# A graph network's last block: seven phases with barriers against one block of tile and chunk pipelines

## The reference, cut to what matters

```python
def _L3_gnn_ref(x, ...):                     # x here is h of the line below
    def _bn(x, gamma, beta):                 # over all nodes
        m = jnp.mean(x, axis=0)
        v = jnp.mean((x - m) ** 2, axis=0)
        return gamma * (x - m) * jax.lax.rsqrt(v + EPS) + beta
    def _hconv(x, src, dst, ew, w1, b1, w2, b2, g, b):
        h = jax.nn.relu(x @ w1 + b1)
        msg = ew[:, None] * h[src]
        agg = jax.ops.segment_sum(msg, dst, num_segments=x.shape[0])
        return jax.nn.relu(_bn(agg @ w2 + b2, g, b))
    residual = x
    h = _hconv(x, src, dst, hyperedge_weight, c1_w1, c1_b1, c1_w2, c1_b2, c1_g, c1_b)
    h = jax.nn.relu(_bn(h, bn1_g, bn1_b))
    h = _hconv(h, src, dst, hyperedge_weight, c2_w1, c2_b1, c2_w2, c2_b2, c2_g, c2_b)
    return jax.nn.relu(_bn(h, bn2_g, bn2_b) + residual)

x = x + _L2_gnn_ref(h, L2_gnn_weight, src, dst, edge_type_8, edge_weight)   # its sum over edges: relation aggregation
h = jnp.maximum(_layernorm(x, axis=-1), 0.0)
return x + _L3_gnn_ref(h, ...)
```

## Time and profile before

| | us |
|---|---|
| median of 3 runs | 4792.98 (4786.26 to 4800.61) |
| the profiled execution | 4766.33 |
| its span, first to last instruction | 4764.6 |
| mean granted TensorE clock, share of full speed | 0.704 |

### The profile page before, as it was taken

How to read it: one execution, slowest core, us unless ns; L and a number is a source line. 1 busy time by engine, 2 the same in 40 slices (tenths; PEclk the granted TensorE clock), 3 DMA queues, 4 the chain that set the end, 5 groups by cost and what they waited for, 6 DMA issues and landing times. The chain is left out here.

```text
span 4764.6 us, 64771 instructions
## 1 busy us (share of the span) xinstructions
PE 2346.9 (49%) x11287; PEld 1706.3 (36%) x11288; DVE 2095.4 (44%) x5420; ACT 1410.0 (30%) x4630; POOL 2382.3 (50%) x2445
## 2 busy tenths in 40 slices
PE   5301646566441155565565725555445555355555
PEld 2201534444330144444443313333323343233343
DVE  6502974444330089444447613335223333233344
ACT  2101746666530165666666600000200002000002
POOL 4774015555547500455553466663466660566660
PEclk9655977777665598777777956667666667666667
DMA  3443433333234344233325733331233330323320
GB/s 111 125 107 92 128 108 95 99 103 96 68 92 119 108 118 125 85 105 99 99 76 134 247 93 92 91 90 49 91 88 88 91 91 19 109 83 91 91 85 29
DMA packets 339577, 465.57 MB, mean 98 GB/s; under 512 B 108191, under 2 KB 253928, under 8 KB 336112
## 3 DMA queue, kind: packets, MB, share of 16 engines
q0 software_dynamic: 113824, 289.70, 21.3%
q1 hardware_dynamic: 157536, 109.12, 8.1%
q10 hardware_dynamic: 67956, 64.45, 4.8%
HBM read 385.88 MB, written 76.97 MB: 97 GB/s over the span
## 5 line engine op out<-in xcount | busy, mean ns | idle before, releaser
L153 POOL DMA_INDIRECT ring<-feat_d,srcC x784 | 755.3, 963 | 1065.2 <-ACTq L167 830.9
L153 POOL DMA_INDIRECT agc_ring<-feat_d,srcC x784 | 742.3, 947 | 614.6 <-SPq L312 234.9
L301 PE MATMUL agc_ps<-agc_ring,agc_hot 128*128 x1760 | 589.0, 500 | 594.2 <-issue 278.3
L175 ACT ACTIVATE ring<-ring,exC 128x64 f32<-128x64 f32 x3136 | 818.1, 336 | 137.1 <-issue 136.3
L301 PE MATMUL bank<-ring,arena 128*128 x1760 | 644.7, 502 | 114.3 <-ACT ring L175 46.7
L301 PEld LDWEIGHTS agc_ps<-agc_ring,agc_hot 128*128 128x128 f32 x1760 | 428.0, 254 | 755.1 <-issue 680.1
L910 PE MATMUL wide<-arena 128*128 128x100 bf16 x4704 | 273.9, 215 | 464.9 <-issue 253.2
L509 POOL DMA_INDIRECT attr_d<-abuf,attr_pos x392 | 406.8, 1038 | 191.2 <-issue 129.1
L228 DVE TENSOR_TENSOR acc<-acc,agc_ps 128x256 f32 x440 | 184.4, 419 | 685.7 <-DMA c1p_bias<-in_L_gnn_c_b 418.5
L153 POOL DMA_INDIRECT agr_ring<-rel_d,relC x392 | 371.3, 947 | 221.9 <-issue 107.9
L301 PEld LDWEIGHTS bank<-ring,arena 128*128 128x128 f32 x1760 | 400.9, 253 | 195.3 <-issue 141.8
(11 more groups left out here) (278 smaller groups left out, 2510.1 us busy)
## 6 DMA issues: line engine op xcount, KB each, us to landing
arena<-lo_d ACTq DMA_DIRECT2D x392, 128.0 KB
rel_d<-mid_stage SPq DMA_DIRECT2D x25, 1024.0 KB, 4.5
arena<-attr_d SPq DMA_DIRECT2D x98, 260.0 KB
abuf<-in_attr SPq DMA_DIRECT2D x56, 448.0 KB
ring<-feat_d,srcC POOLq DMA_INDIRECT x784
agc_ring<-feat_d,srcC POOLq DMA_INDIRECT x784
feat_d<-arena ACTq DMA_DIRECT2D x50, 128.0 KB
attr_d<-abuf,attr_pos POOLq DMA_INDIRECT x392
```

Of the source, the lines that this page charges most:

```text
L153: pool.indirect_dma_start(out=ring[:, u % RING, j, 0:D], out_offset=None, in_=table, in_offset=bass.IndirectOffsetOnAxis(ap=index[:, u, j: ...
L175: last = act.activation(part_of_row, part_of_row, ACT.Copy, scale=exC[:, bass.ds(u, 1), j, h])
L301: last = pe.matmul(ps[k % NHOT][:, 0:g.width], hot[:, k % NHOT, j, :], ring[:, slot, j, 0:g.width], start=(j == 0), stop=(j == 1))
```

## The change

Everything behind the middle stage becomes one function `tail()` with a single block, in which each engine runs one program from the relation aggregation to the output:

- The middle stage ends with DVE clearing `acc`; before the second convolution's aggregation POOL clears it, once its tiles have been turned. The relation aggregation adds its steps straight into `X`.
- All weights of both convolutions are loaded at the start of the block, by 16 DMAs of SP, and `AT` and `G` lie in the ring of the gathers.
- Layer norm, turn and the first projection form a pipeline by tile: each engine handles a different tile at a time, with two or three buffers between. The square root gets its epsilon as bias and is done per tile.
- A projection has a third matmul, of a row of ones (one contraction row) and the bias row, and ACT rectifies out of PSUM into the stage. DVE has no part in it.
- The convolution is a pipeline by chunk of 4 tiles (512 columns; 7 chunks, the last of one tile). ACT copies the turned even tiles and DVE the odd ones; ACT evicts, DVE takes the statistics of a chunk as soon as it is evicted. Normalisation is done chunk by chunk, with statistics, the next projection or the turning back behind it.
- At the output the drain goes and the two DVE operations of neighbouring tiles alternate.

The core of the diff (the functions `layer_norm`, `to_feature_major`, `conv_project`, `conv_finish` and the output block are removed):

```diff
                         dve.drain()
+                    dve.memset(acc[:, :, 0:D], 0.0)
 
     middle()
     end_phase()
+        CH = [(4 * r, min(4 * r + 4, NT)) for r in range(-(-NT // 4))]
+        AT = ring_flat[:, 0:KD * NP].rearrange("p (c n) -> p c n", c=KD)
+        G = ring_flat[:, KD * NP:2 * KD * NP].rearrange("p (c n) -> p c n", c=KD)
+        pt = [psum(f"t_pt{k}", [P, 512]) for k in range(2)]
+        pf = [psum(f"t_pf{k}", [P, 512]) for k in range(2)]
...
+        def act_rectify(act, z, n):
+            act.wait_ge(s_proj, NT * z + n + 1)
+            wait_from(act, stored[n % 5], 16 * (5 * z + n // 5))
+            act.activation(stage[:, n % 5, :], pf[n % 2][:, 0:D], ACT.Relu).then_inc(s_relu, 1)
+
+        def pe_project(pe, z, n, source):
+            wait_from(pe, s_relu, NT * z + n - 1)
+            pe.matmul(pf[n % 2][:, 0:D], ones[:, :], b1[:, z, :], start=True, stop=False)
+            for c in range(KD):
+                last = pe.matmul(pf[n % 2][:, 0:D], source(c), W1[:, z, c, :], start=False, stop=(c == KD - 1))
+            last.then_inc(s_proj, 1)
+
+        def dve_normalise(dve):
+            for j in range(NT + 1):
+                if j < NT:
+                    dve.bn_stats(stats[:, j, :], X[:, j, :])
+                if 1 <= j <= NT:
+                    dve.wait_ge(s_root, j)
+                    dve.reciprocal(rstd[:, j - 1:j], rstd[:, j - 1:j])
+                dve.drain()
+                if j < NT:
+                    dve.bn_aggr(mv[:, j, :], stats[:, j, :]).then_inc(s_var, 1)
+                if 1 <= j <= NT:
+                    dve.scalar_tensor_tensor(out=shift[:, j - 1:j], in0=mv[:, j - 1, 0:1], scalar=-1.0,
+                                             in1=rstd[:, j - 1:j], op0=ALU.mult, op1=ALU.mult).then_inc(s_shift, 1)
+                dve.drain()
+
+        def act_normalise(act):
+            for j in range(NT + 4):
+                if j < NT:
+                    act.wait_ge(s_var, j + 1)
+                    act.activation(rstd[:, j:j + 1], mv[:, j, 1:2], ACT.Sqrt, bias=eps[:, 0:1]).then_inc(s_root, 1)
+                if 1 <= j <= NT:
+                    n = j - 1
+                    act.wait_ge(s_shift, n + 1)
+                    act.activation(HB[:, n, :], X[:, n, :], ACT.Relu, bias=shift[:, n:n + 1],
+                                   scale=rstd[:, n:n + 1]).then_inc(s_norm, 1)
+                if 2 <= j <= NT + 1:
+                    n = j - 2
+                    act.wait_ge(s_ht, n + 1)
+                    wait_from(act, s_proj, n - 1)
+                    act.copy(ht[:, n % 2, :], pt[n % 2][:, 0:D]).then_inc(s_htc, 1)
+                if j >= 4:
+                    act_rectify(act, 0, j - 4)
...
+        def pe_convolve(pe, z):
+            def chunk(r):
+                a0, a1 = CH[r]
+                pe.wait_ge(s_ata[z], -(-a1 // 2))
+                pe.wait_ge(s_atd[z], a1 // 2)
+                for c in range(KD):
+                    if r:
+                        pe.wait_ge(s_g[z], KD * (r - 1) + c + 1)
+                    for a in range(KD):
+                        last = pe.matmul(pf[c][:, 0:(a1 - a0) * P], W2[:, z, a, c * P:(c + 1) * P],
+                                         AT[:, a, a0 * P:a1 * P], start=(a == 0), stop=(a == KD - 1))
+                    last.then_inc(s_p[z], 1)
+
+            pe.wait_ge(g_conv[z].added, T + NHOT)
+            for r, (a0, a1) in enumerate(CH):
+                for n in range(a0, a1):
+                    if n >= 2:
+                        pe.wait_ge((s_ata, s_atd)[n % 2][z], n // 2)
...
+                if r:
+                    chunk(r - 1)
+            chunk(NR - 1)
...
+        def act_convolve(act, z):
...
+            for r, (a0, a1) in enumerate(CH):
+                for n in range(a0, a1):
+                    if n % 2 == 0:
+                        copy_turned(act, act.copy, z, n)
+                if r:
+                    evict(r - 1)
+            evict(NR - 1)
...
+        def act_sqrt(act, z, q):
+            act.wait_ge(s_coef[z], 2 * q + 1)
+            act.activation(bsc[:, :, 0], bmv[:, :, 1], ACT.Sqrt, bias=eps[:, 1:2]).then_inc(s_sqrt[z], 1)
+            act.wait_ge(s_coef[z], 2 * q + 2)
...
+        def dve_convolve(dve, z):
+            for r, (a0, a1) in enumerate(CH):
+                for n in range(a0, a1):
+                    if n % 2:
+                        copy_turned(dve, dve.tensor_copy, z, n)
+                if r:
+                    dve_stats(dve, s_g[z], r - 1)
+            dve_stats(dve, s_g[z], NR - 1)
+            dve_coefs(dve, z, 0)
+            for r in range(NR):
+                dve_stats(dve, s_n1[z], r)
+            dve_coefs(dve, z, 1)
...
+                gather_pairs(pool, g_rel, rel_d, relC, ring)
+                for z in range(2):
+                    if z:
+                        pool.wait_ge(s_at[0], NT)
+                        pool.memset(acc[:, :, 0:D], 0.0).then_inc(s_zero, 1)
+                    for k in range(5):
+                        pool.wait_ge(stored[k], 16 * 5 * (z + 1))
+                    gather_pairs(pool, g_conv[z], feat_d, srcC, ring)
...
+                    for r in range(NR):
+                        act_norm(act, z, 1, r, s_n2[z], ACT.Identity if z else ACT.Relu)
+                        if z == 0 and r >= 2:
+                            for n in range(*CH[r - 2]):
+                                act_rectify(act, 1, n)
...
+                add_steps(dve, "agr", g_rel, hot, ps, X)
...
+                for n in range(NT + 1):
+                    if n < NT:
+                        dve.wait_ge(s_back, n + 1)
+                        wait_from(dve, s_out, n - 2)
+                        dve.tensor_tensor(tmp[:, n % 3, :], pt[n % 2][:, 0:D], HB[:, n, :], ALU.add).then_inc(s_sum, 1)
+                    if n >= 1:
+                        k = n - 1
+                        dve.wait_ge(s_sum, k + 1)
+                        dve.scalar_tensor_tensor(out=X[:, k, :], in0=tmp[:, k % 3, :], scalar=0.0, in1=X[:, k, :],
+                                                 op0=ALU.max, op1=ALU.add).then_inc(s_out, 1)
```

More of the change, by code:

```diff
@@ L1464, in _ @@
             @block.vector
             def _(dve):
-                with dve.Fori(0, NT) as n:
-                    dve.bn_stats(stats[:, n, :], X[:, n, :])
+                dve.memset(ones[:, :], 1.0)
+                dve.memset(eps[:, 0:1], LN_EPS)
+                dve.memset(eps[:, 1:2], BN_EPS).then_inc(s_eps, 1)
+                add_steps(dve, "agr", g_rel, hot, ps, X)
                 dve.drain()
-                for n in range(NT):
-                    dve.bn_aggr(mv[:, n, :], stats[:, n, :])
@@ L1684, in gnn_program @@
[L1684 to L1689 removed]
+                dve.wait_ge(s_w, 16 * 16)
+                dve_normalise(dve)
+                for z, tag in enumerate(convs):
+                    if z:
+                        dve.wait_ge(s_zero, 1)
+                    add_steps(dve, f"ag{tag}", g_conv[z], hot, ps, acc)
+                    dve_convolve(dve, z)
@@ L1703, in _ @@
-            def _(dve):
-                with dve.Fori(0, 5) as i:
-                    for k in range(5):
-                        n = 5 * i + k
-                        dve.wait_ge(s_t, n + 1)
-                        dve.tensor_tensor(tmp[:, k, :], pt[k][:, 0:D], HB[:, n, :], ALU.add)
-                        dve.drain()
-                        dve.scalar_tensor_tensor(out=X[:, n, :], in0=tmp[:, k, :], scalar=0.0,
-                                                 in1=X[:, n, :], op0=ALU.max, op1=ALU.add).then_inc(s_x, 1)
@@ L1713, in _ @@
[L1713 to L1722 removed]
+                multiply_steps(pe, "agr", g_rel, ring, hot, ps)
@@ L1723, in gnn_program @@
+                for r, (a0, a1) in enumerate(CH):
+                    pe.wait_ge(s_n2[1], KD * (r + 1))
+                    for n in range(a0, a1):
+                        wait_from(pe, s_sum, n - 1)
+                        for c in range(KD):
+                            last = pe.transpose(pt[n % 2][:, c * P:(c + 1) * P], G[:, c, n * P:(n + 1) * P],
+                                                ident[:, :])
+                        last.then_inc(s_back, 1)
+    tail()
     life.close()
```

352 lines of the change are left out of this document (139 added, 213 removed).

## The result

| | before | after |
|---|---|---|
| median of the runs, us | 4793.9 (10 runs, 4786.3 to 4821.9) | 4820.7 (10 runs, 4806.1 to 4829.0) |
| ratio after to before | | 1.0048, 95% interval 1.0029 to 1.0066 |
| profiled execution, us (span) | 4766.33 (4764.6) | 4825.47 (4823.6) |
| mean granted TensorE clock | 0.704 | 0.704 |

The forecast was 4737 us, range 4708 to 4772. The change costs about 27 us instead: the medians are 26.8 us apart, and the interval of the ratio lies above 1.

A forecast was written before the change was run, and what follows sets the result against it. Bound: in the aggregations, the chain of steps holding up gathers; in B, D and E, engines working one after another. Gains 27.7 + 8.2 + 20.3 = 56.2 us; 56 off the 4792.98 median gave 4737 us, range 4708 to 4772.

The forecast's parts named there:

- the price of the bias matmul in B: Two more matmul records a tile in B: between nothing (hidden) and 0.43 us, the full 0.43 taken.
- B: Stage after the relation aggregation (add, layer norm, turn, projection): 51 us instead of 78.7, bounds 45 and 66.
- D: Stage after the first convolution's aggregation (turn, convolution, two batch norms, projection): 93.5 us instead of 101.7.
- a rise after PE's pause: Low tensor clock at the start of the projections: adds 2 us in B, 2.6 in D.
- the clock at 0.50 in B: Sign of being wrong; expected was a granted clock near 1.00 from 5 us into each PE run.
- Rival 3: Low tensor clock through the fused stages, from pauses between interleaved PE work: 64 us slower, 4857 us; chance 0.05.
- point of decision: In Rival 3: beyond 47% of the fused PE time at the low clock, the change loses.
- E: Stage after the second convolution's aggregation (like D without projection, then the output): 81.2 us instead of 101.5.
- The aggregations: Three gathering stages (relations, first and second convolution): change of 0, at most 10 us gained in all.
- rival 2: Aggregations shorten too, their chain starting 3 to 4 us earlier: 4727 us, or 4721 if clearing held gathers; chance 0.13.
- my sign of 5 us: Sign of being wrong: an aggregation that changes by over 5 us; 588 +- 3 us was expected.
- Rivals 1 and 4: First: queue order eats half, 4757 to 4777 us, chance 0.18. Other: boundaries go without overlap, 4768 us, chance 0.06.

The follow-up runs named there:

- set 1: First follow-up runs, on one chip: the change with 128-row, zero-padded or no bias matmul, and the kernel before with a one-row one; kernel before there 4762.7 us.

## Why the prediction was wrong, step by step

**The step that failed** is the price of the bias matmul in B, and with it in D: "between nothing and 2 x 0.216 = 0.43 I take the full 0.43, as a record here goes by its columns". The measured price against no bias at all is 57.1 us in B (96.9 less 39.8), 2.28 a tile, and 53.0 in D, 2.12 a tile: five times the upper bound. The price has three parts; the last two are estimates from the pace of a tile, and the three sum to 59 and 55 us. The plain cost of two more records, seen with 128 rows, is 7.2 us in B and 9.2 in D, 0.29 and 0.37 a tile: this is what I had priced, and 0.43 was a fair figure. The second is the clock. A tile of B takes 1.515 us with 128 rows, twice that is 3.03, and the pace in after was 3.58; D's projection takes 1.295, twice 2.59, and 3.15 in after. So the low clock costs 1.5 and 1.3 a tile, some 38 and 32 us. The third is the remainder, 0.55 us a tile at the low clock (0.38 measured at the high one), 14 us in each. I put it down to the weight loads laid bare where the number of rows changes: in after too they start with their matmuls. A 128-row tile at the low clock exists in one place, the second of D's projection with 128 rows, and took 2.52 us, near the doubled 2.59. I had written that the trace has no such shape, and then bounded the unknown by rows of another shape, in time only. The bound should have asked what else such an instruction may change for its neighbours.

**The clock.** I gave B and D's projection 2 to 2.6 us for a rise after PE's pause, from the earlier trace rows. With 128 rows that is what happened (B at a mean clock of 0.96). In the kernel after the sign that I had named for being wrong came, "the clock at 0.50 in B". Rival 3 is the case that came: its effect in B and D's projection, not in the convolution nor by the cause that I gave it (pauses), and it had a chance of 0.05. Its prices were 84 for B and 63.5 for D's projection; the row changes made them 96.9 and some 79. Its point of decision held: of PE's 245 busy us in the three stages, 90 in B and 79 in D's projection passed at the low clock, and 16 at the output, where DVE sets the pace. The first two are over two thirds of the time, against the 47% at which the change was to lose, and it lost; counted as work, a low microsecond for half, they are some 55%, so it was nearer than it looks. What spoke against it for me, "at full queue the clock came back after 5 us", was a reading of full-row matmuls alone.

**The rest of B.** Forecast 51, measured 47.0 with 128 rows; 1.7 a tile against 1.52. PE was the slowest, not ACT's queue. The table load of 1.28 us ahead of ACT's first root was not in the sum. The kernel before has one too, but there it lay beneath other work. Without it the chain took the 3.6 us as written.

```profile
3334.30 1.28 ACT L1544 ACT_TABLE_LOAD   x1 [602.71 <-DVE mv L1534]
```

**D.** To the first coefficients 35.7 against 39 (PE idle 5.5 us in all, not 8 + 1), coefficients 1.8 against 2.2, normalisation to the second coefficients 11.5 against 11.8, and the projection, with 128 rows, at exactly the 1.3 a tile: 88.6 against 93.5. The lines of after that answer to the earlier trace rows:

```profile
4059.74 0.55 DVE L1636 BATCH_NORM_AGGREGATE t_bmv<-t_bn 128x2 f32<-128x42 f32 x2
...
4061.56 9.37 ACT L1620 ACTIVATE t_ring<-t_ring,t_bsc 128x512 f32<-128x512 f32 x14 [0.94 <-DVE t_bsc L1645]
4062.41 8.77 DVE L1631 BATCH_NORM_STATS2 t_bn<-t_ring 128x6 f32<-128x512 f32 x14 [0.89 <-ACT t_ring L1620]
...
4073.07 4.35 ACT L1620 ACTIVATE t_ring<-t_ring,t_bsc 128x512 f32<-128x512 f32 x6 [0.94 <-DVE t_bsc L1645]
...
4074.65 1.22 PE L1520 MATMUL t_pf<-t_b,t_ones 1*128 1x256 f32 x2 [15.64 <-ACT t_ring L1620]
```

ACT's 14 pieces took 9.37 us (forecast 9.2) with the statistics beneath. POOL's clearing, forecast at 5.5 us and covered, took 5.44 at 4054.14 and ended nearly 97 us ahead of the gathers.

**E.** 75.0 against 81.2: the same 3 us in the convolution, and the output at the pace of DVE's two operations, 0.67 a tile instead of 0.78, although PE's clock there is 0.50 (the windows at 4787 and 4799): PE is not what the stage waits for, as DVE is busy for 15.04 of 16.0 us.

```profile
4814.48 0.42 DVE L1735 TENSOR_TENSOR t_tmp<-t_pt,HB 128x256 f32<-128x256 f32 x1
...
4815.15 0.42 DVE L1735 TENSOR_TENSOR t_tmp<-t_pt,HB 128x256 f32<-128x256 f32 x1
```

**The aggregations.** Zero stands for the forms compared on one chip. In set 1 they took 589.2, 591.2 and 587.7 with 128 rows, against 588.3, 591.4 and 589.2 in the kernel before with one row, which keeps its clearing and its late start. The first add now comes 2 to 4 us sooner and the clearing is gone: rival 2 gave nothing. The first profile of after, with 596.2, 593.7 and 592.2, went over my sign of 5 us in two of three; its cause is open. That the chain of steps holds up the gathers fits the chips of the result and of set 1 only. On the other two an aggregation takes 497 us, and the gathers follow each other at 1.25 us to the end: the 490 us that I had worked out for gathers that nothing holds. Rivals 1 and 4 did not show in the 128-row form: no queue order cost more than forecast.

**Without the one step**, with 128 rows, the three stages sum to 210.7 where 225.7 was forecast, and the gain on the kernel before was 72 us where 56 was. The other steps were close or on the careful side (B, D and E each came out 4 to 6 us below the forecast); the one that missed was an operation of a shape that the trace did not hold.

## What to carry to other kernels

Don't add a bias by an fp32 matmul with one contraction row in each tile of a stage that PE bounds: spread it over all 128 rows (1/128 times the value, or zeros in the other rows), which took 88 us less here, or let an engine add it that is idle there. When a trace shows PE busy without a gap and the granted clock at 0.50, look at the row counts of its matmuls before its waits. And a new instruction form is priced with its effect on its neighbours (clock, cover of the weight loads), or its upper bound is not a bound.

## What the runs showed of the hardware

- Stages that alternate one-row with 128-row fp32 matmuls stayed at 1.2 GHz with PE busy all the time (80 of 80 us in B, 74 of 74 in D's projection); with 32 rows B took the same 96.9 us. The same with 128 rows rose to 2.4 GHz, and rows of zeros did as well (B 46.6 and 47.0).
- The effect depends on the past: once at 2.4 GHz, after four tiles with full rows, the one-row stage stayed there to its end.
- Each pair of changes of the row count went with 0.38 us more a tile at 2.4 GHz (1.90 against 1.52) and, by an estimate from doubled tiles, 0.55 at 1.2; the weight load next to each change started with its matmul and not before it.
- PE with a quarter of its time idle in B rose to 2.4 GHz and held it (31.05 of 42 us busy), while with full-row transposes of 128 columns at the output it stayed at 1.2 GHz (15.2 of 16.0 us busy).
- The same programs took about 1130 us less on two of the three chips, 91 us of it in each of the three aggregations of this block. In set 1 and in the profiles of the result, DVE stands idle for over 5 us some 23 to 28 times in the relation aggregation, often near 10 us and with POOL gathering on at 1.25 us, as in this row of after; on the others at most once, and the chain is one of gathers. Why the chips differ is open; no run was made on it.

```profile
2774.07 0.42 DVE L228 TENSOR_TENSOR X<-X,t_ps 128x256 f32 x1 [9.57 <-issue]
```

- Also open: at how many rows between 32 and 128 the clock rises; whether it is the few rows that keep it low or the changes of the row count with their bare weight loads, as no run parts the two; and why it stays low at the output.
